# Attention scores and value sums in one tile shape of TensorE: 64 rows by 32 columns, with the value sums in two PSUM banks

## The reference

```python
q, k, v = split_heads(x @ Wq), split_heads(x @ Wk), split_heads(x @ Wv)
attn = einsum('bhsd,bhtd->bhst', q, k) * scale + pos_bias
attn = softmax(attn, axis=-1)
out = einsum('bhst,bhtd->bhsd', attn, v)
```

## Time and profile before

| what | value |
|---|---|
| median of 3 runs | 3097.91 us (3089.46 to 3098.75) |
| profiled execution, its own time | 3101.1 us |
| span of that execution | 3099.0 us |
| mean granted TensorE clock | 0.978 |

### The profile page before, as it was taken

The page is one execution under the profiler, slowest core; times in us unless marked ns, Lnnn a source line. Parts: engine busy times, 40 slices in busy tenths (PEclk is TensorE's granted clock), DMA queues, the critical chain, the costliest instruction groups (busy, mean ns, idle before and its releaser), DMA issues. The chain is left out here.

```text
span 3099.0 us, 55504 instructions
## 1 busy us (share of the span) xinstructions
PE 2879.0 (93%) x21844; PEld 869.9 (28%) x21844; DVE 636.0 (21%) x798; ACT 2696.4 (87%) x2867; POOL 766.7 (25%) x1420
## 2 busy tenths in 40 slices
PE   6957999999999999999999999999999996699998
PEld 3531222222222222222222222222222222355555
DVE  4750111111111111111111111111111111655441
ACT  3747999999999999999999999999999994466664
POOL 0221333333323232323333333323232321000000
PEclk9988999999999999999999999999999998799999
DMA  4441111111111111111111111111111101110100
GB/s 105 159 166 37 27 27 27 27 32 35 30 31 29 30 27 27 30 27 27 27 27 27 27 27 34 34 28 30 30 30 27 27 6 29 43 44 24 40 30 21
DMA packets 166069, 117.34 MB, mean 38 GB/s; under 512 B 111318, under 2 KB 156212, under 8 KB 165108
## 3 DMA queue, kind: packets, MB, share of 16 engines
q1 hardware_dynamic: 163780, 107.50, 12.6%
q0 software_dynamic: 2048, 6.43, 0.6%
HBM read 67.42 MB, written 47.75 MB: 37 GB/s over the span
## 5 line engine op out<-in xcount | busy, mean ns | idle before, releaser
L706 ACT ACTIVATE pr<-ps 128x1179 f32<-128x1179 f32 (+1 forms) x2176 | 2292.4, 1139 | 71.7 <-PE ps L650 46.2
L670 PE MATMUL ps<-pr,va 128*32 128x393 f32 x12800 | 1393.8, 507 | 0.0
L626 POOL TENSOR_TENSOR pr<-pr,e_cur 128x310 f32<-128x310 f32 (+19 forms) x1344 | 704.4, 535 | 1656.6 <-ACT pr L706 1622.7
L650 PE MATMUL ps<-qa,ka 48*128 48x393 f16 (+12 forms) x3808 | 700.5, 319 | 93.7 <-DMA qa<-right_rows 38.6
L647 PE MATMUL ps<-qa,ka 51*128 51x393 f16 (+18 forms) x3360 | 628.0, 316 | 22.0 <-ACT pr L706 11.7
L717 DVE COPY o_sb<-ps 128x393 f32<-128x393 f32 x64 | 36.4, 568 | 2089.0 <-PE ps L670 2089.0
L670 PEld LDWEIGHTS ps<-pr,va 128*32 128x32 f32 x12800 | 252.6, 108 | 476.3 <-issue 453.4
L650 PEld LDWEIGHTS ps<-qa,ka 48*128 48x128 f16 x3808 | 189.7, 94 | 675.3 <-ACT pr L706 514.4
L647 PEld LDWEIGHTS ps<-qa,ka 51*128 51x128 f16 (+1 forms) x3360 | 167.0, 94 | 688.0 <-ACT pr L706 684.0
L1401 PE MATMUL ps<-ln_all,w 128*128 128x393 f32 x512 | 180.1, 494 | 4.9 <-ACT hid L1461 4.9
L1461 ACT ACTIVATE hid<-ps,b 128x393 f32<-128x393 f32 x256 | 135.4, 587 | 54.6 <-PE ps L1401 54.1
(11 more groups left out here) (117 smaller groups left out, 938.2 us busy)
## 6 DMA issues: line engine op xcount, KB each, us to landing
qa<-q_halves SPq DMA_DIRECT2D x64, 196.5 KB
ka<-k_halves SPq DMA_DIRECT2D x64, 196.5 KB
att_rows<-o_norm SPq DMA_DIRECT2D x64, 196.5 KB, 2.2
ln_rows<-ln SPq DMA_DIRECT2D x32, 196.5 KB, 3.5
q_halves<-halves SPq DMA_DIRECT2D x32, 196.5 KB, 2.7
k_halves<-halves SPq DMA_DIRECT2D x32, 196.5 KB, 3.6
qa<-q_halves SPq DMA_DIRECT2D x64, 98.2 KB
ka<-k_halves SPq DMA_DIRECT2D x64, 98.2 KB
```

The costliest lines, as they stand in the source:

```text
L626: nc.gpsimd.tensor_tensor(p, p, e_cur[0:keys, par, t:t + z - a], ALU.mult).then_inc(s_band, 1)
L650: last = nc.tensor.matmul(out[:, cut:W], ka[r:r + 48, par, k0:k0 + keys], qa[r:r + 48, par, q0 + cut:q0 + W], start=True, stop=True, tile_ ...
L670: last = nc.tensor.matmul(ps[quad:quad + 32, O_PS + side, 0:W], va[0:keys, par, kt], pr[0:keys, g % SLOTS_PR, j], start=(kt == 0), stop=(k ...
L706: nc.scalar.activation(pr[:, g % SLOTS_PR, 0:m], ps[:, 3 * (g % 2):3 * (g % 2) + m, 0:W], ACT.Exp, scale=1.0 / (LIFT * LIFT)).then_inc(s_e ...
```

## The change

Both kinds of matmul use tiles of 64 rows by 32 columns. A unit's scores are four matmuls instead of one, each for 32 keys, in four column tiles (a split unit's eight instead of two). A unit's value product is two matmuls of 64 keys each, at rows 0 and 64; the lower keys sum in bank 6, the upper keys in bank 7. DVE adds the two banks when it drains a side. The next side uses the same two banks, so its first batch waits for the addition; that batch is put two groups later in the order, where three batches follow one another. The key tile of 65 keys is filled with zeros on the value side (more memsets ahead of the attention).

```diff
                 def scores(k, g):
...
-                        if cut > 0:
-                            last = nc.tensor.matmul(out[:, 0:cut], ka[r:r + 51, par, k0:k0 + keys], qa[r:r + 51, par, q0:q0 + cut],
-                                                    start=True, stop=True, tile_position=(r, 0))
-                        if cut < W:
-                            last = nc.tensor.matmul(out[:, cut:W], ka[r:r + 48, par, k0:k0 + keys], qa[r:r + 48, par, q0 + cut:q0 + W],
-                                                    start=True, stop=True, tile_position=(r, 0))
+                        for x in range(0, keys, 32):
+                            y = min(x + 32, keys)
+                            if cut > 0:
+                                last = nc.tensor.matmul(out[x:y, 0:cut], ka[r:r + 51, par, k0 + x:k0 + y], qa[r:r + 51, par, q0:q0 + cut],
+                                                        start=True, stop=True, tile_position=(r, x))
+                            if cut < W:
+                                last = nc.tensor.matmul(out[x:y, cut:W], ka[r:r + 48, par, k0 + x:k0 + y], qa[r:r + 48, par, q0 + cut:q0 + W],
+                                                        start=True, stop=True, tile_position=(r, x))
...
                 def values(k, m):
...
-                        pe.wait_ge(s_o[side], at(2 * k + par))
-                    for u in batches[m]:
...
-                        last = nc.tensor.matmul(ps[quad:quad + 32, O_PS + side, 0:W], va[0:keys, par, kt], pr[0:keys, g % SLOTS_PR, j],
-                                                start=(kt == 0), stop=(kt == KT - 1), tile_position=(0, quad))
+                        pe.wait_ge(s_o, at(4 * k + 2 * par + side))
+                    for half in range(2):
+                        r = 64 * half
+                        for u in batches[m]:
...
+                            last = nc.tensor.matmul(ps[quad:quad + 32, O_PS + half, 0:W], va[r:r + 64, par, kt], pr[r:r + 64, g % SLOTS_PR, j],
+                                                    start=(kt == 0), stop=(kt == KT - 1), tile_position=(r, quad))
...
-                HEAD = 3
+                HEAD = 5
...
-                        while done < NB and group_of[batches[done][-1]] <= g - DELAY:
+                        while done < NB and group_of[batches[done][-1]] + 2 * (done % KT == 0) <= g - DELAY:
...
             def _(dve):
...
-                        nc.vector.tensor_copy(o_sb[:, side], ps[:, O_PS + side, 0:W]).then_inc(s_o[side], 1)
-                        dve.wait_ge(s_o[side], at(2 * k + half // 2 + 1))
+                        nc.vector.tensor_copy(o_sb[:, side], ps[:, O_PS, 0:W]).then_inc(s_o_low, 1)
+                        dve.wait_ge(s_o_low, n2 + 1)
+                        nc.vector.tensor_tensor(o_sb[:, side], ps[:, O_PS + 1, 0:W], o_sb[:, side], ALU.add).then_inc(s_o, 1)
+                        dve.wait_ge(s_o, at(n2 + 1))
```

More of the change, by code:

```diff
@@ L514, in build @@
             s_pv = primed(ctx, "f_pv", BATCHES)
-            s_o = [primed(ctx, f"f_o{i}") for i in range(2)]
+            s_o = primed(ctx, "f_o")
+            s_o_low = semaphore(ctx, "f_o_low")
             s_shuf = semaphore(ctx, "f_shuf")
@@ L582, in store_half @@
                     sp.wait_ge(s_norm_o, 2 * n + side + 1)
-                    sp.wait_ge(s_init, 3)
+                    sp.wait_ge(s_init, 6)
                     dst = bass.AP(att_rows, n * (CH * 32 * W) + side * (4 * 32 * W), [[W, P], [1, W]])
@@ L596, in _ @@
                         store_half(2 * k + par, 0)
-                        sp.wait_ge(s_o[1], at(2 * k + par + 1))
-                        sp.wait_ge(s_init, 3)
+                        sp.wait_ge(s_o, at(4 * k + 2 * par + 2))
+                        sp.wait_ge(s_init, 6)
                         load_head(2 * k + par + 2, par)
@@ L613, in _ @@
                 pool.wait_ge(s_init, 2)
-                nc.gpsimd.memset(va[:, :, :, HD:32], 1.0).then_inc(s_init, 1)
+                nc.gpsimd.memset(va[:, :, 0:KT - 1, HD:32], 1.0).then_inc(s_init, 1)
                 pool.wait_ge(s_init, 3)
+                nc.gpsimd.memset(va[64:128, :, KT - 1], 0.0).then_inc(s_init, 1)
+                pool.wait_ge(s_init, 4)
+                nc.gpsimd.memset(va[0:64, :, KT - 1, HD:32], 1.0).then_inc(s_init, 1)
+                pool.wait_ge(s_init, 5)
+                nc.gpsimd.memset(va[64:LAST, :, KT - 1, HD:32], 1.0).then_inc(s_init, 1)
+                pool.wait_ge(s_init, 6)
                 for k in range(NBH // 2):
@@ L629, in _ @@
             def _(pe):
-                pe.wait_ge(s_init, 3)
+                pe.wait_ge(s_init, 6)
                 def scores(k, g):
@@ L663, in values @@
                         pe.wait_ge(s_vld[par], (k + 1) * 48)
-                        pe.wait_ge(s_o[side], at(2 * k + par))
-                    for u in batches[m]:
[L666 to L669, removed]
-                        last = nc.tensor.matmul(ps[quad:quad + 32, O_PS + side, 0:W], va[0:keys, par, kt], pr[0:keys, g % SLOTS_PR, j],
-                                                start=(kt == 0), stop=(kt == KT - 1), tile_position=(0, quad))
+                        pe.wait_ge(s_o, at(4 * k + 2 * par + side))
+                    for half in range(2):
+                        r = 64 * half
+                        for u in batches[m]:
+                            par, kt, c = units[u]
+                            quad = 32 * (c % 4)
+                            g, j = place(u)
+                            last = nc.tensor.matmul(ps[quad:quad + 32, O_PS + half, 0:W], va[r:r + 64, par, kt], pr[r:r + 64, g % SLOTS_PR, j],
+                                                    start=(kt == 0), stop=(kt == KT - 1), tile_position=(r, quad))
                     last.then_inc(s_pv, 1)
-                HEAD = 3
+                HEAD = 5
                 def pair(k, last):
@@ L710, in _ @@
             def _(dve):
-                dve.wait_ge(s_init, 3)
+                dve.wait_ge(s_init, 6)
                 with dve.Fori(0, NBH // 2) as k:
```

## The result

The changed kernel takes 3163.5 us (median of 4 runs, 3160.4 to 3169.5) against 3097.8: ratio 1.022, 95% interval 1.0196 to 1.0245. It is slower where I forecast faster (whether by more than 2% the interval leaves just open), 133 us above the 3030 of the likeliest case and near the upper end of the range.

A forecast was written before the change was run, and what follows sets the result against it. The prediction took ScalarE's exponentials (floor 2208 us) as the limit, delayed by TensorE's shape passages to 2336.6. Floor plus 58 us of stalls left 71 us gain: 3101.1 to 3030 us, range 2965 to 3180.

The forecast's parts named there:

- the likeliest case: Whole kernel: gain of 71 us to 3030 us, own range 3005 to 3060, chance 0.50.
- The passages: TensorE between scores and values: switching tile shape costs about 0.22 us in every 1.23; equal shapes remove it.
- Stream time and feeding: TensorE mid-side: a group's scores plus a batch take 0.93 us, at most 1.02, under 1.033; extra matmuls can be taken in.
- Rival 3: TensorE can't take in a weight load and matmul every 43 ns: 3460 us at 50 ns, 4000 at 60; chance 0.23.
- break-even: TensorE: time per weight load and matmul, 43.3 ns, above which the kernel is slower than before.
- The two prices: TensorE: least spacing of matmul starts, about 25 ns, or about 62 ns when firmware decodes them.
- The addition and its wait: DVE at a side's drain: adding two banks takes 570 ns, hidden; the next side's first batch need not wait.
- The cover of 2 us: At a side's start: time left of four exponentials, 4.1 us, after last batch, copy and addition, about 2.1 us.
- Moved: the order at a side's start: Scores of group 8 stand behind three batches of 1.98 us: a stall of 0.8 us a side.
- ScalarE's floor: Exponentials at 1.033 us, those of two units at 0.72: 2208 us in all, 138.0 for a pair of heads.
- the short groups at a side's end: Two groups want scores every 0.72 us while a batch lies between: 0.1 us more a side.

The follow-up runs named there:

- the two kernels that change one part: Scores alone in 64 by 32 against the kernel before, 3121.5 us; values alone in 64 by 32 with two banks, without deferral, 3112.9 us.
- the kernel that nothing but ScalarE holds: Changed kernel with each side's first batch no longer put two groups later: 3005.0 us, ratio 0.972; a second time 3002.2 us, 0.971.

## Why the prediction was wrong, by its steps

**The passages: right.** The 0.22 us a batch goes entirely once both shapes agree. The trace of the changed kernel shows 1.03 us between exponentials in the middle of sides, and the two kernels that change one part show the price still there. "TensorEngine Tiling (Array Packing)" of the Trainium skill, Key Properties, gave this cause, a drain at a change of tiling mode, and the runs agree: the price comes and goes with the difference of mode.

**Stream time and feeding: right.** A batch and a group's scores fit into an exponential. Rival 3, the largest of the others with 0.23, did not come about. In the kernel with added work a dense stretch is this:

```profile
788.87:790.78 1.91, 1.91 (x96) 1.22 (x100) 1.88 (x4) 1.91 (x3) 0.00 (x0) 1.00 0.00 0
```

96 matmul records fall into 1.91 us, and 92 of them start there, 21 ns each; the break-even was 43.3. The two prices that the prediction took from "TensorE: Matmul & The Clock Gate" of the Trainium skill, 62 and 25 ns, are both above what this stretch shows. (The prediction's "2.4 times over anything in the trace", under rival 3, doesn't come out of its rows: 112 ns against 40.9 is 2.7 times, and 72 ns of rows 7 against 40.9 is 1.8.) Instruction traffic is 7.23 MB (7.3 foretold) and costs nothing that is seen.

**The addition and its wait: right.** VectorE's new instruction takes 569 ns (570 taken), and no first batch waits for it. The cover of 2 us was ample; without the deferral almost none is left, and still nothing is lost. Whether the deferral itself could be spared, the prediction did not ask.

**The step that failed: "Moved: the order at a side's start".** I found the right place, exponential 8, and the right mechanism, scores behind three batches, and priced it with 3 x 0.66 us at the upper clock: a stall of 0.8 us, bounds 0 to 1.3. (With its own 0.36 us for the scores of group 7 the sum gives 0.9.) It is 2.5 us (3.56 between two starts, less 1.03). I had counted what TensorE does after the deferral and not what it does during it: four groups of scores alone, about 0.3 us of stream in each 1.03. The granted clock, which I had read as 1.00 and taken for given, is a result of how TensorE is loaded: the same order with 64 more matmuls a side keeps it at 1.00. The Trainium skill ("TensorE: Matmul & The Clock Gate", "A second HAM failure mode: psum-queue depth-cycling") tells of a kernel that loses the clock by frequent short idles between groups of matmuls. The trace agrees: here no pause was longer than 0.53 us, and the clock fell all the same. No rival of mine had this mechanism. Where the clock holds, in the kernel with added work, the stall is 0.9 us (3060 us - 3003 us = 57 us over 64 sides), so the order of events was priced right to 0.1 or 0.2.

**A second term, mis-sized: ScalarE's floor.** I took 1.033 us, the spacing of neighbours after a pause, for its lasting pace. That gave 138.0 us for a pair of heads; the kernel that nothing but ScalarE holds takes (2484.1 - 242.1 + 0.9) / 16 = 140.2, with 0.9 for its last exponential. That is 2.2 x 16 = 35 us less gain. The 0.1 us that I had put on the short groups at a side's end belongs here as well. The hint stood in rows 4, where three records in a row grow from 1.15 to 1.18 us.

The sum again with the measured terms: 16 x 140.2 = 2243 for ScalarE, 64 x 2.5 = 160 for the stalls, together 2403; from the first start, 247.3, to the end of the last exponential, 2649.3, it took 2402. Predicted were 2266: 35 us of the 136 by the floor, about 100 by the clock. The split is good to some 10 us, since the floor is that of another kernel. In the changed kernel itself the starts stay 1.033 apart to the end of a side, and most of ScalarE's term is paid behind the two short groups: 0.88 and 0.97 us instead of 0.72, 0.41 us a side, 26 us.

## What to carry to other kernels

If scores and values alternate on TensorE, give them the same tile rows and the same tile columns; half an adaptation buys nothing. When work is put off to cover a wait, look at what is left in the stretch from which it is taken: a stretch that is sparse for a few microseconds can cost the clock just when the work put off arrives, and the wait that it covered may be cheaper. And take an engine's pace from a long undisturbed run of it, not from the first neighbours.

## Not expected of the hardware

- TensorE's granted clock fell to the lower level for 3.4 us after 4 us in which the engine was busy 2.42 of 3.98 us by the records, with no pause over 0.53 us. 64 added matmuls a side kept it up and saved 103 us.
- The same order in the old shapes held the clock down for 6.8 us at 36 of 63 sides. With at most two batches in a row it fell at 39 of 64 sides and not at the others.
- Starts of exponentials can run ahead of the engine: 1.033 us apart at first, with records that grow from 1.15 to 1.45 us over 24 of them, then 1.047. A busy row from start to end hides it; the length of the records shows it.
- TensorE started 92 matmuls, each with its weight load, in 1.91 us with eight tiles in use, 21 ns a pair, over far more than one batch.
